# xDeepFM-style recommender on one core: first spread of the next pair ahead, row-sums in front of spreads, reordered first pairs, gathers without a wait for layouts

## What is computed

```
emb = tables[feat, sparse]                       # 512 x 26 x 32, a gather
linear = lin_sparse_w[feat, sparse].sum(-1) + dense @ lin_dense_w
xk = emb
for w, b in (conv1 (128 x 26*26), conv2 (128 x 64*26)):
    hp = xk[:, h, d] * emb[:, m, d]  for all h, m         # outer product per sample and d
    xn = sigmoid(w @ hp + b)                     # 128 x 32 per sample
    xk, res = xn[:, :64], xn[:, 64:]             # conv2 needs only its res half
cin  = concat(res1, res2).sum(-1) @ cin_w + cin_b
deep = tanh(tanh(tanh([emb, dense] @ W1 + b1) @ W2 + b2) @ W3 + b3) @ deep_w + deep_b
out  = linear + cin + deep + bias                # 512 numbers
```

## Time and profile before

| | |
|---|---|
| median of three runs | 473.79 us |
| profiled execution | 473.68 us, its span 471.6 us |
| PE busy | 429.2 us, 91% |
| DVE busy | 319.9 us, 68% |
| ACT busy | 162.8 us, 35% |
| POOL busy | 149.4 us, 32% |
| DMA | 64.00 MB, 136 GB/s in the mean |
| mean granted clock of TensorE | 0.96 |

### The profile page before, as it was taken

How to read it: one execution, slowest core, us unless ns; L and a number is a source line. 1 busy time by engine, 2 the same in 40 slices (tenths; PEclk the granted TensorE clock), 3 DMA queues, 4 the chain that set the end, 5 groups by cost and what they waited for, 6 DMA issues and landing times.

```text
span 471.6 us, 4901 instructions
## 1 busy us (share of the span) xinstructions
PE 429.2 (91%) x1716; PEld 181.0 (38%) x1716; DVE 319.9 (68%) x356; ACT 162.8 (35%) x264; POOL 149.4 (32%) x146
## 2 busy tenths in 40 slices
PE   3586969969899999999999999999999989999998
PEld 3532312313333333333333333333333323888685
DVE  3109456578697797989797797979797797332111
ACT  3151151341533454352544454352533330111111
POOL 6515633060505051432406051334000074860000
PEclk9878887979999999999999999999999989999999
DMA  5475643727677676777776596786665560420000
GB/s 178 107 155 136 142 107 81 188 57 190 136 178 172 157 196 165 171 186 182 174 189 168 151 213 155 169 191 166 164 177 129 141 178 0 113 68 1 0 0 0
DMA packets 38302, 64.00 MB, mean 136 GB/s; under 512 B 19601, under 2 KB 22033, under 8 KB 38278
## 3 DMA queue, kind: packets, MB, share of 16 engines
q1 hardware_dynamic: 34694, 61.93, 52.7%
q0 software_dynamic: 3584, 1.76, 2.8%
HBM read 61.96 MB, written 1.71 MB: 135 GB/s over the span
## 4 chain that ended last, share of the span: by engine, by line
PE 80%; DVE 10%; issue 8%; ACT 1%; DMA 0%; DVEq 0%
PE conv L430 37%; PE conv L408 19%; PE ring L420 7%; PE conv L486 7%; PE ring L486 7%; DVE prod L689 5%; DVE copied L689 3%; PE ring L394 2%; ACT sq L528 0%; DMA idx_sb<-in_idx 0%; ACT xk L539 0%; DVE x L623 0%; PE conv L505 0%; PE conv L501 0%; PE conv L437 0%
## 5 line engine op out<-in xcount | busy, mean ns | idle before, releaser
L346 POOL DMA_INDIRECT emb<-in_table,rows x112 | 115.2, 1029 | 207.0 <-DMA laid<-emb 175.5
L689 DVE TENSOR_TENSOR prod<-ring,xk 128x1024 f32<-128x1024 f32 x112 | 133.0, 1217 | 64.9 <-PE ring L420 32.6
L430 PE MATMUL conv<-prod,w_sb 128*64 128x512 f32 x448 | 116.9, 637 | 0.2
L689 DVE TENSOR_TENSOR copied<-copied,xk 128x1024 f32<-128x1024 f32 x96 | 116.1, 1250 | 0.3
L430 PE MATMUL conv<-copied,w_sb 128*64 128x512 f32 x384 | 93.6, 607 | 2.9 <-DVE copied L689 2.9
L408 PE MATMUL conv<-sq,w_sb 117*128 117x512 f32 x192 | 93.0, 622 | 0.5 <-ACT res L541 0.5
L539 ACT ACTIVATE xk<-conv,const_sb 64x512 f32<-64x512 f32 x64 | 43.8, 684 | 125.2 <-PE conv L408 115.6
L528 ACT ACTIVATE sq<-ring 117x512 f32<-117x512 f32 x96 | 52.0, 597 | 61.0 <-PE ring L394 52.8
L420 PE MATMUL ring<-x,sel_sb 58*128 58x512 f32 x224 | 48.8, 479 | 13.3 <-DVE prod L689 11.5
L408 PEld LDWEIGHTS conv<-sq,w_sb 117*128 117x128 f32 x192 | 34.8, 194 | 57.9 <-issue 56.5
L430 PEld LDWEIGHTS conv<-copied,w_sb 128*64 128x64 f32 x384 | 28.0, 141 | 62.6 <-issue 51.8
(11 more groups left out here) (75 smaller groups left out, 293.4 us busy)
## 6 DMA issues: line engine op xcount, KB each, us to landing
copied<-laid SPq DMA_DIRECT2D x192, 256.0 KB
wpiece<-in_mlp SPq DMA_DIRECT2D x22, 256.0 KB
emb<-in_table,rows POOLq DMA_INDIRECT x112
raw<-laid SPq DMA_DIRECT2D x32, 52.0 KB
laid<-emb SPq DMA_DIRECT2D x16, 96.0 KB, 4.5
sel_f<-in_sel SPq DMA_DIRECT2D x1, 832.0 KB, 5.7
const_sb<-in_const SPq DMA_DIRECT2D x1, 626.0 KB, 4.1
w_sb<-in_w SPq DMA_DIRECT2D x1, 416.0 KB
```

The lines of the kernel that those rows point to most:

```text
L346: pool.indirect_dma_start(out=emb[0:n, i, j, :], out_offset=None, in_=table, in_offset=bass.IndirectOffsetOnAxis(ap=rows[0:n, i, j:j + 1], ...
L430: mm = nc.tensor.matmul(conv[i % 2][c * HALF:(c + 1) * HALF, :], w2_sb[:, t, :], prod_of(r)[:, c, :], start=(t == 0), stop=(t == T2 - 1))
L689: nc.vector.tensor_tensor(prod_of(r)[:, :, :].rearrange("p c n -> p (c n)"), left[:, :, :].rearrange("p c n -> p (c n)"), xk[i % 2][:, :, ...
```

## The change

- PE's order: in front of the mains of a group, the row-sums now come before the spreads. `SPREADS_IN` names the spreads; the first spread of the next pair moves from the last group to the third, and the second stays in the last one.
- The first pairs: `SUMS_IN`, `L1_IN`, `X_LOW_AT` and `FOLD1_AT` have three entries in place of four, so that pair 2 already has the order of all later pairs; ACT's order of squares and sigmoids follows that.
- The start: 100 useless matmuls instead of 60. A row-sum of half 0 waits for `x_low` of that half only. ACT squares all of half 0 first, then half 1, and PE does the first half of layer 1 ahead of the first two spreads.
- SP: lay_out(1) and fetch(1) come after two copies instead of five, lay_out(2) and fetch(2) one copy earlier. POOL's gathers no longer wait for the layout of the pair before; they wait only for the gather of four pairs before.

```diff
+SPREADS_IN = (((0, 4), (0, 5)), ((0, 8), (0, 9)), ((0, 12), (1, 0)), ((1, 1),))
 SUMS_IN = ({1: ((1, 0), (1, 1)), 2: ((1, 2),)},
-           {0: ((1, 0), (1, 1)), 1: ((1, 2),), 3: ((2, 0),)},
-           {0: ((1, 1), (1, 2)), 3: ((2, 0), (2, 1))},
+           {0: ((1, 0), (1, 1)), 1: ((1, 2),), 2: ((2, 0),), 3: ((2, 1),)},
            {0: ((1, 2),), 2: ((2, 0),), 3: ((2, 1),)})
-L1_IN = ({2: 0, 3: 1}, {1: 0, 2: 1}, {1: 0, 2: 1}, {0: 0, 1: 1})
-X_LOW_AT, TURN_AT, FOLD1_AT, PIECE_AT = (12, 11, 9, 5), (9, 9, 9, 9), (5, 5, 7, 7), 11
-WARM = 60
+L1_IN = ({2: 0, 3: 1}, {1: 0, 2: 1}, {0: 0, 1: 1})
+X_LOW_AT, TURN_AT, FOLD1_AT, PIECE_AT = (12, 7, 5), 9, (5, 5, 7), 11
+WARM = 100
...
-            return [(i + ahead, u) for ahead, u in SUMS_IN[min(i, 3)].get(g, ()) if i + ahead < NPAIR]
+            return [(i + ahead, u) for ahead, u in SUMS_IN[min(i, 2)].get(g, ()) if i + ahead < NPAIR]
...
-            if g + 1 < len(GROUPS):
-                return [T2 * i + t for t in GROUPS[g + 1] if t in SPREAD]
-            return [T2 * (i + 1) + t for t in GROUPS[0] if t in SPREAD and i + 1 < NPAIR]
+            return [T2 * (i + ahead) + t for ahead, t in SPREADS_IN[g] if i + ahead < NPAIR]
+
+        def squares_up_to(i, u, c):
+
+            return UT * c + u + 1 if i == 0 else 2 * (UT * i + u) + c + 1
...
             for g in range(len(GROUPS)):
+                for j, u in sums_in(i, g):
+                    enter(("sums", j, u))
                 for r in spreads_in(i, g):
                     enter(("spread", r))
-                for j, u in sums_in(i, g):
-                    enter(("sums", j, u))
...
             fetch(0)
-            for n in range(RC):
+            for n in range(2):
                 copy(n)
             lay_out(1)
             fetch(1)
+            for n in range(2, RC):
+                copy(n)
...
-                    if i == 0 and k == 1:
+                    if i == 0 and k == 0:
                         lay_out(2)
                         fetch(2)
...
             def gather(i):

-                if i:
-                    pool.wait_ge(laid_in[(i - 1) % RX], LAID * ((i - 1) // RX + 1))
                 if i >= GSEM:
                     pool.wait_ge(rows_in[i % GSEM], ROWS * (i // GSEM))
...
-                if u == 0:
-                    pe.wait_ge(x_lo_done, 2 * (i + 1))
                 slot_free("sums", i, u)
                 for c in range(2):
                     at = HALF * c
+                    if u == 0:
+                        pe.wait_ge(x_lo_done, 2 * i + c + 1)
...
+            pe.wait_ge(w1_step, 4)
+            layer1(0, 0)
             pe.wait_ge(sel_done, 2)
             spread_tile(0)
             spread_tile(1)
-            pe.wait_ge(w1_step, 4)
-            layer1(0, 0)
             layer1(0, 1)
...
                 for g, tiles_now in enumerate(GROUPS):
+                    for j, u in sums_in(i, g):
+                        sums_of(j, u)
                     for r in spreads_in(i, g):
                         spread_tile(r)
-                    for j, u in sums_in(i, g):
-                        sums_of(j, u)
...
             x_high(0)
-            for u in range(UT):
-                squares(0, u)
+            for c in range(2):
+                for u in range(UT):
+                    act.wait_ge(sums_done, u + 1)
+                    nc.scalar.activation(sq[0][0:UK, u, c, :], sums_bank(0, u)[0:UK, c, :], ACT.Square).then_inc(sq_done, 1)
...
-                    for u in range((0, 1)[i - 1] if i < 3 else 2, UT):
+                    for u in range(0 if i == 1 else 2, UT):
                         squares(i + 1, u)
-                if i == 1:
-                    sigmoid(2, 0)
                 if i + 2 < NPAIR:
                     x_high(i + 2)
                 if i <= KW:
                     piece_high(i - 1)
                 if i + 1 < NPAIR:
-                    for c in range(1 if i == 1 else 0, 2):
-                        sigmoid(i + 1, c)
+                    sigmoid(i + 1, 0)
+                    sigmoid(i + 1, 1)
                 if i + 2 < NPAIR:
-                    for u in range(1 if i == 1 else 2):
-                        squares(i + 2, u)
+                    squares(i + 2, 0)
+                    squares(i + 2, 1)
```

More of the change, by code:

```diff
@@ L240, in build @@
             enter(("sums", 0, u))
-        for r in spreads_in(-1, len(GROUPS) - 1):
-            enter(("spread", r))
+        for t in range(2):
+            enter(("spread", t))
         for i in range(NPAIR):
             for g in range(len(GROUPS)):
+                for j, u in sums_in(i, g):
+                    enter(("sums", j, u))
                 for r in spreads_in(i, g):
                     enter(("spread", r))
-                for j, u in sums_in(i, g):
-                    enter(("sums", j, u))
         def l1_bank(i, c):
@@ L384, in slot_free @@
                 else:
-                    pe.wait_ge(sq_done, 2 * (UT * last[1] + last[2]) + 2)
+                    pe.wait_ge(sq_done, squares_up_to(last[1], last[2], 1))
             def sums_of(i, u):
-                if u == 0:
-                    pe.wait_ge(x_lo_done, 2 * (i + 1))
                 slot_free("sums", i, u)
@@ L406, in layer1 @@
                 for u in range(UT):
-                    pe.wait_ge(sq_done, 2 * (UT * i + u) + c + 1)
+                    pe.wait_ge(sq_done, squares_up_to(i, u, c))
                     mm = nc.tensor.matmul(l1_bank(i, c)[:, :], w1_sb[:, u, :], sq[i % 2][0:UK, u, c, :],
@@ L455, in _ @@
                 for g, tiles_now in enumerate(GROUPS):
+                    for j, u in sums_in(i, g):
+                        sums_of(j, u)
                     for r in spreads_in(i, g):
                         spread_tile(r)
-                    for j, u in sums_in(i, g):
-                        sums_of(j, u)
                     for t in tiles_now:
                         main(T2 * i + t)
-                    if g in L1_IN[min(i, 3)] and i + 1 < NPAIR:
-                        layer1(i + 1, L1_IN[min(i, 3)][g])
+                    if g in L1_IN[min(i, 2)] and i + 1 < NPAIR:
+                        layer1(i + 1, L1_IN[min(i, 2)][g])
             pe.wait_ge(lin_step, 1)
@@ L692, in _ @@
                                             ALU.mult).then_inc(prod_done, 1)
-                    k = min(i, 3)
+                    k = min(i, 2)
                     if i == 0 and t == 3:
@@ L699, in _ @@
                         fold1_of(i)
-                    if t == (0 if i == NPAIR - 1 else TURN_AT[k]):
+                    if t == (0 if i == NPAIR - 1 else TURN_AT):
                         turn(i)
-                    if t == TURN_AT[k] and i:
+                    if t == TURN_AT and i:
                         fold2_of(i - 1)
```

## The result

The changed kernel took 446.02 us (median of four runs, 444.75 to 448.0) against 473.78 before; the ratio is 0.9418, 95% interval 0.9383 to 0.9452. Two later groups of runs of the same kernel gave 444.97 and 587.1 us: in some groups the kernel with gathers back to back takes 140 us more, a danger that no step of the prediction names. The experiments come to it.

The account below looks back on a forecast made before the run. The prediction took the kernel as PE-bound with holes. Gains of 13.7 (start and first pairs), 9.5 (settled pairs) and 1.5 (end) sum to 24.7, so 473.68 - 24.7 = 449.0 us; 8-in-10 range 443.5 to 459.

Parts of the forecast that it names:

- first term: Start through pair 2: main(12) of pair 3 at 130.1 against 143.82, 13.7 us gained.
- The start: Longer warm-up, layer 1 before spreads, squares and sums by half: product 0 at 31.9 instead of 34.34, 2.4 us gained.
- Gathers: Gathers back to back on POOL: lay_out(1) near 24; only cover for the next part, no gain in the other 12 pairs.
- Pairs 0 to 2: New order in the first pairs: main(12) of pair 2 at 109.7 instead of 123.39, including 4.6 us charged for clock falls.
- new wait of row-sum (3,1): End of pair 1: the sum needs the squares of (3,0), which ACT does after layer 1's sigmoids; a 3.3 us hole.
- Rival (c): First pairs gain only in pair 0, pairs 1 and 2 stay at 27 us: 8 us back, 457; 12%.
- Spread 0 ahead: Pairs 3 to 14: first spread of the next pair goes earlier, removing 0.87 us idle PE a pair, 9.5 us.
- Rival (b): The settled pairs' wait only moves (product 8's spread, late raw, squares): 9.5 us back, 458.5; 12%.
- The end: Last pair, paced by DVE: product 1 is ready with main(12) of pair 14, 1.5 us gained.
- Rival (a): The clock holds in pairs 1 and 2: 4.6 us less, 444.4; 18%.
- Rival (d): Slower: gathers without a break slow every copied product in pairs 0 to 6, by 1.06 us each: 475.4; 3%.

Follow-up runs that it names:

- experiment 12: The changed kernel, unaltered, run a third time as control beside the old kernel with free gathers: 444.97 us.
- experiment 1: Changed kernel with both first spreads of the next pair in the last group again: 458.41 us.
- experiment 4: Changed kernel, but each gather waits for the layout of the pair before it again: 445.93 us.
- experiment 11: Kernel before, with one part alone: gathers do not wait for layouts: 473.49 us, ratio 1.000.
- experiment 6: Changed kernel, but SP issues all five copies of pair 0 ahead of the layout and fetch of pair 1: 588.56 us.
- experiment 7: Changed kernel with the squares of row-sum (3,0) ahead of the second sigmoid of pair 2 on ACT: 584.9 us.
- experiment 8: Changed kernel with the third row-sum and both layer-1 halves of the next pair one group earlier in pairs 0 and 1: 582.15 us.
- experiment 10: Changed kernel with gathers waiting for layouts, third row-sum and layer 1 a group earlier in pairs 0 and 1, layout of pair 4 two copies earlier: 439.93 us.
- experiment 2: Kernel before, with only spread 0 of the next pair moved from the last group to the third: 462.84 us, ratio 0.9767.
- experiment 9: The changed kernel, unaltered, again: 587.1 us, with the crawl (PE and ACT hardly get an instruction done for 140 us).

## Why the prediction was right

Right in size: 449.0 against 448.0 for the profiled execution, by terms 13.7 + 9.5 + 1.5 = 24.7, measured 143.82 - 130.40 = 13.4, then 233.82 - 223.96 = 9.9 (main(12) of pair 3 to pair 14), and 19.64 - 17.51 = 2.1 (to pair 15, before at 397.28), together 25.4 of the 25.7 measured. Within the first term two misses of about 1.2 us cancel, which is luck. Step by step:

- *The start.* Forecast 2.4 us, measured 34.34 - 33.15 = 1.2. The 100 matmuls ended at 20.35, not 23.0, because they took 0.119 us each and not 0.144. x came 1.0 us later than in the earlier trace rows, and the hole of 1.41 us cost the clock for layer 1 (4.51 us instead of 2.8). "Without a hole" was the wrong part. The step came as forecast where the clock held: experiment 12, the same kernel, had no hole at all, and product 0 started 30.17 - 21.19 = 8.98 us after the first row-sum, 8.9 in the forecast (9.70 in experiments 1 and 4, with holes of 0.80 and 0.58 us).
- *Gathers.* "Only the cover" holds by experiments 4 and 11: no time is lost or won by them. The layout of pair 1 was forecast at 24 and went out at 26.16, that of pair 3 at 52 and 52.54.
- *Pairs 0 to 2.* Pair 0 (product 0 to product 0) forecast 26.8, measured 27.1; pair 1 23.1 and 2.3 for the clock, measured 25.35; main(12) of pair 2 forecast 109.7, measured 110.00. The clock fell behind both holes, as charged, but not alike: the four mains behind the first took 5.85 us (3.58 at full clock), those behind the second 4.22. So pair 2 took 24.4 us from product 0 to main(12) and not 23.3 + 2.3, and that made up for the late start. The new wait of row-sum (3,1) for the squares stands in the trace at 3.30 us, as worked out. Experiments 6 to 8 and 10 show what it and the late layer 1 still cost: 1.0 to 1.5 us for the wait alone, 7.1 to 7.6 with layer 1 a group earlier. Rival (c) is refuted by main(12) of pair 2.
- *Spread 0 ahead.* 20.40 us a pair, forecast 20.43; experiment 1 takes it away and experiment 2 gives it. x_low did wait longer (in the earlier trace rows ACT waited 2.46 us for raw, now 3.12 at 197 us), within the margin. Rival (b) is refuted.
- *The end.* 2.1 us against 1.5, product 1 as forecast, and less lost beside POOL's subtractions: two copied products took 2.35, 3.57 and 3.61 us where the old ones took 4.46, 3.52 and 2.34.
- *Rival (a)*, the clock holds in pairs 1 and 2, is refuted for the profiled execution, and for that of experiment 12 (445.26 us), where the four mains behind the first hole took 4.96 us. The other three runs (444.75 to 446.09) had a mean clock of 0.988 to 0.992 against 0.981; in which stage they had more of it, no trace shows.
- *Rival (d)* as told is refuted: between 36 and 144 us, beside gathers without a break, copied products take 1.22 us in the mean, as in the kernel before. The Trainium skill's rule on the shared port ("SBUF — State Buffer", section "Who interferes with whom") shows here only beside POOL's subtractions. But the words "gathers without a break" named what is now the main suspect, with the wrong mechanism: the price, where it comes, is 140 us, and it falls on PE and ACT. No run shows a product slowed by gathers. The 3% for slower left this out.

## What to carry to other kernels

When a queue of steady pairs loses a little at each seam, move the first producer of the next pair ahead of the last consumers of this one: one spread was worth 11 us. In a ring of few buffers, read for each entry which older entry it waits for, and check the same for the engine that frees it; both large holes of the first pairs, and the new one, were read off that way. A wait that costs nothing can still pace an engine: taking it away brought no time here and, by all that the runs show so far, a danger of 140 us, so keep it unless its removal pays.

## What the runs showed of the hardware

- The crawl above, in experiment 9: from 18 us PE slows to one instruction in 2.80 us, and ACT does none from 20 us until 162, 18 us after the last of 112 gathers without a pause, at a DMA share of 0.11 from 100 to 120 us; in two groups of runs and not in the three others.
- The granted clock reads 1.00 from the first warm-up matmul on, yet from 9 to 11 us only 12 to 15 of them run in 2 us, and from 13 us on 19 to 21. The two rows of experiment 1's kernel:

```profile
9.00:11.00 2.00, 2.00 (x12) 2.00 (x11) 0.33 (x1) 0.06 (x1) 1.70 (x2) 1.00 0.13 17
...
13.00:15.00 2.00, 2.00 (x20) 2.00 (x20) 0.00 (x0) 0.00 (x0) 1.53 (x2) 1.00 0.11 13
```

So the mean of 60 matmuls that include the first stretch (0.144 us) did not hold for 100 (0.119 us in the changed kernel, 0.132 in experiment 1). What slows the first ones, at a recorded clock of 1.00, is not shown.
